# A graph network with cross-attention: a new order of VectorE's steps in the attention units, and of the three engines' steps in the openings

## The reference

```python
h = relu(layernorm(x)); x_in = h
h = batchnorm(h); h = gcn(h, gcn_in_w)              # 1024 nodes, 512 wide, 16384 edges
for i in range(4):
    a = attn(ln2(h), cond, Wq[i], Wk[i], Wv[i], Wo[i])   # 16 batches of 64 nodes, 256 keys each, 8 heads of 64
    h = h + a
    val, gate = split(ln3(h) @ geglu_w[i] + geglu_b[i])
    h = h + (val * gelu(gate)) @ ffo_w[i] + ffo_b[i]
return x + gcn(h, gcn_out_w) + x_in
```

## Time and profile before

| | |
|---|---|
| runs | 2527.58, 2528.76, 2528.82 us; median 2528.76 us |
| profiled execution | 2525.96 us, of which the span from first to last instruction is 2522.8 us |
| mean granted TensorE clock | 0.982 |
| busy: TensorE, its weight loads, VectorE, ScalarE, GpSimd | 2362.4, 2066.8, 1691.1, 1248.3, 1075.6 us |

### The profile page before, as it was taken

How to read it: one execution, slowest core, us unless ns; L and a number is a source line. 1 busy time by engine, 2 the same in 40 slices (tenths; PEclk the granted TensorE clock), 3 DMA queues, 4 the chain that set the end, 5 groups by cost and what they waited for, 6 DMA issues and landing times.

```text
span 2522.8 us, 38407 instructions
## 1 busy us (share of the span) xinstructions
PE 2362.4 (94%) x14270; PEld 2066.8 (82%) x14270; DVE 1691.1 (67%) x3027; ACT 1248.3 (49%) x2585; POOL 1075.6 (43%) x730
## 2 busy tenths in 40 slices
PE   7888899899999999899999999899999999899999
PEld 5367888888888889888888889888887989888887
DVE  9985666676656666686656666686666666686554
ACT  9954656654333555654333555653333555553322
POOL 3136755646643322346643322346553322346530
PEclk9999999999999999999999999999999999999999
DMA  2042333312231333212231333212231333212231
GB/s 76 1 168 89 141 121 121 122 33 69 59 120 45 105 104 118 92 34 67 59 122 51 101 100 118 93 34 67 60 121 58 99 95 118 92 38 63 63 121 42
DMA packets 115880, 214.53 MB, mean 85 GB/s; under 512 B 9520, under 2 KB 71600, under 8 KB 113904
## 3 DMA queue, kind: packets, MB, share of 16 engines
q1 hardware_dynamic: 115408, 207.89, 24.9%
q10 hardware_dynamic: 288, 4.19, 0.4%
HBM read 176.13 MB, written 35.91 MB: 84 GB/s over the span
## 4 chain that ended last, share of the span: by engine, by line
PE 69%; DVE 19%; ACT 6%; issue 4%; POOL 2%; DMA 0%; DVEq 0%; ACTq 0%; POOLq 0%
PE ps L2350 8%; PE ps L2352 8%; PE ps L2351 8%; PE ps L2719 6%; PE ps L2723 6%; PE ps L2721 6%; PE ps L2599 6%; PE ps L2602 6%; PE ps L2601 6%; DVE qbd L2028 2%; DVE kv L2005 2%; DVE o_full L2043 2%; PE ps L2913 1%; PE ps L2627 1%; DVE qbd_b L2028 1%
## 5 line engine op out<-in xcount | busy, mean ns | idle before, releaser
L2599 PE MATMUL ps<-wv_hi,cb 128*128 128x256 f32 x896 | 259.6, 290 | 6.7 <-DVE kv L2005 3.8
L2599 PE MATMUL ps<-cb,wk_hi 128*128 128x256 f32 x896 | 261.3, 292 | 4.6 <-POOL cb L803 2.9
L2601 PE MATMUL ps<-cb,wk_hi 128*128 128x256 f32 x896 | 257.1, 287 | 0.0
L2602 PE MATMUL ps<-cb,wk_lo 128*128 128x256 f32 x896 | 256.7, 286 | 0.0
L2601 PE MATMUL ps<-wv_lo,cb 128*128 128x256 f32 x896 | 256.3, 286 | 0.0
L2602 PE MATMUL ps<-wv_hi,cb 128*128 128x256 f32 x896 | 256.2, 286 | 0.0
L823 POOL TENSOR_TENSOR v_lo<-kv,v_hi 128x512 fp32r<-128x512 f32 x96 | 125.3, 1305 | 292.3 <-ACT v_hi L1260 292.0
L878 POOL TENSOR_TENSOR f_lo<-ff,f_hi 128x512 fp32r<-128x512 f32 x128 | 168.9, 1331 | 172.2 <-ACT f_hi L1504 172.1
L2283 DVE TENSOR_TENSOR h<-h,ps 128x512 f32<-128x512 f32 x256 | 168.3, 683 | 59.7 <-PE ps L2352 59.7
L2352 PE MATMUL ps<-wf_hi,f_lo 128*128 128x512 f32 x512 | 199.2, 389 | 0.0
L2350 PE MATMUL ps<-wf_hi,f_hi 128*128 128x512 f32 x512 | 199.2, 389 | 0.0
(11 more groups left out here) (377 smaller groups left out, 6984.5 us busy)
## 6 DMA issues: line engine op xcount, KB each, us to landing
cb<-cb_s SPq DMA_DIRECT2D x168, 512.0 KB, 4.6
stage<-in_pieces SPq DMA_DIRECT2D x256, 128.0 KB, 2.6
cb_s<-cb SPq DMA_DIRECT2D x56, 512.0 KB, 2.6
stage<-in_pieces SPq DMA_DIRECT2D x44, 512.0 KB, 3.6
stage<-in_condT SPq DMA_DIRECT2D x7, 1024.0 KB, 5.8
stage<-in_pieces SPq DMA_DIRECT2D x16, 256.0 KB, 3.4
at_s<-at_hi ACTq DMA_DIRECT2D x2, 2048.0 KB, 11.7
wo_raw<-in_pieces SPq DMA_DIRECT2D x8, 512.0 KB, 4.6
```

What stands on the lines that cost most here:

```text
L2599: pe.matmul(to, l_hi, r_hi, start=(fresh and i == 0 and k == 0), stop=False, skip_group_check=True)
L2601: pe.matmul(to, l_hi, r_lo, start=False, stop=False, skip_group_check=True)
L2602: last = pe.matmul(to, l_lo, r_hi, start=False, stop=(k == 1), skip_group_check=True)
```

## The change

It moves instructions, and adds or removes none in the groups. Four parts:

1. In the groups VectorE does `q_low` before `kv_five` (before, it did it after `kv_late` 1 and `o_part`), and `pT_low` before the maxima in place of behind them. In the last group `o_low` comes ahead of the reciprocal.
2. In the openings all four `first_x2_low` of both halves are VectorE's. GpSimd's part of them is gone; it waits on `x2_ok` before it takes up its larger pieces.
3. For layers 1 to 3 the sums and the higher part of V1 move from the end of the MLP into the opening (VectorE: ahead of `first_z2` of use 1; ScalarE: behind `q_copy(0, 1)`). In layer 0 the same places hold V0, and GpSimd's lower part of it comes before `kv_low` 1 and 2.
4. On TensorE the last four transposes of use 1 come ahead of key step 5; `kv_late` 1 and 2 follow the lower parts on VectorE.

Besides, in the first graph convolution two of three small copies (`take_picked`) come ahead of the sums of the second key weight.

```diff
 # GpSimd, layer 0, before the layers
-            for j in range(2, BLOCKS):
+            for j in range(2, 5):
+                cond_low(0, j)
+            pool.wait_ge(x2_ok, FIRST)
+            for j in range(5, BLOCKS):
                 cond_low(0, j)
 # GpSimd, opening
-                for k in range(2):
-                    first_x2_low(0, k)
-                kv_low(l, 0, KEYS, 0)
                 first_rsqrt(2 * l + 1)
                 pool.wait_ge(z2_ok, 2 * FIRST * l + 2 * FIRST)
...
+                kv_low(l, 0, KEYS, 0)
                 zero_q()
-                for k in range(2):
-                    first_x2_low(1, k)
+                pool.wait_ge(x2_ok, 2 * FIRST * l + 2 * FIRST)
+                if l == 0:
+                    attn_low(VALUES, 0, 0)
                 for n in range(1, 3):
                     kv_low(l, 0, KEYS, n)
-                if l == 0:
-                    attn_low(VALUES, 0, 0)
                 attn_low(VALUES, 1, l)
 # ScalarE, opening
-                for p in range(1, 3):
-                    q_copy(0, p)
+                q_copy(0, 1)
                 if l == 0:
-                    attn_high(VALUES, 0, 0)
-                q_copy(0, 3)
+                    act.wait_ge(c_lo, BLOCKS)
+                attn_high(VALUES, int(l > 0), l)
+                q_copy(0, 2)
+                act.wait_ge(q_mm, 2 * FIRST * l + FIRST)
                 for k in T2_ORDER[1]:
                     first_x2_high(1, k)
+                q_copy(0, 3)
 # ScalarE, end of the MLP
                     wq_high(l + 1)
-                    attn_high(VALUES, 1, l + 1)
 # VectorE, value_units
                     if t:
+                        q_low(t, 1)
                         o_part(u - 2, 2)
                     kv_five(t, VALUES)
                     kv_11_low(t, VALUES)
+                    pT_low(u)
                     maxima(u + 1)
                     kv_late(t, VALUES, 0)
                     softmax(u + 1)
                     kv_late(t, VALUES, 1)
-                    pT_low(u)
                     if t:
                         o_part(u - 1, 3)
-                        q_low(t, 1)
                     kv_late(t, VALUES, 2)
+                    pT_low(u + 1)
                     maxima(u + 2)
-                    pT_low(u + 1)
 # VectorE, key_units (the same for pT_low)
+                    if last:
+                        o_low(GROUPS * l + t - 1)
                     softmax(u)
-                    if t:
+                    if t and not last:
                         o_low(GROUPS * l + t - 1)
...
                     o_part(u - 2, 0)
                     if not last:
+                        q_low(t + 1, 0)
                         kv_five(t + 1, KEYS)
                     if t:
                         residual(t - 1, GROUPS * l + t - 1)
                     if not last:
                         kv_11_low(t + 1, KEYS)
+                    pT_low(u)
+                    if t:
+                        z3_of(t - 1, GROUPS * l + t - 1)
                     maxima(u + 1)
...
-                        q_low(t + 1, 0)
                         kv_late(t + 1, KEYS, 2)
 # VectorE, opening
-                for k in range(2, KC):
+                for k in range(KC):
                     first_x2_low(0, k)
...
+                attn_sums(VALUES, int(l > 0), l)
                 first_z2(2 * l + 1, range(FIRST))
-                if l == 0:
-                    attn_sums(VALUES, 0, 0)
                 for k in T2_ORDER[1][:3]:
                     first_x2_full(1, k)
-                kv_late(0, KEYS, 1)
+                for k in T2_ORDER[1][:2]:
+                    first_x2_low(1, k)
                 first_x2_full(1, 2)
                 for k in T2_ORDER[1][2:]:
                     first_x2_low(1, k)
-                kv_late(0, KEYS, 2)
-                for i in range(2):
-                    q_low(0, i)
+                for n in range(1, 3):
+                    kv_late(0, KEYS, n)
+                q_low(0, 0)
                 if l == 0:
                     attn_sums(VALUES, 1, 0)
+                q_low(0, 1)
 # VectorE, end of the MLP
-                    if q == MG - 1 and l < L - 1:
-                        attn_sums(VALUES, 1, l + 1)
 # TensorE, opening
                 q_product(0, 3)
-                kv_step(0, KEYS, 5)
                 first_t2(1, T2_ORDER[1][3:])
-                kv_step(0, KEYS, 6)
+                for j in range(5, BLOCKS):
+                    kv_step(0, KEYS, j)
```

More of the change, by code:

```diff
@@ L853, in _ @@
             pool.wait_ge(z2_ok, FIRST)
-            for j in range(2, BLOCKS):
+            for j in range(2, 5):
+                cond_low(0, j)
+            pool.wait_ge(x2_ok, FIRST)
+            for j in range(5, BLOCKS):
                 cond_low(0, j)
             for l in range(L):
-                def first_x2_low(use, k):
-                    pool.wait_ge(full2_ok, 2 * FIRST * l + t2_place(use, k) + 1)
-                    pool.wait_ge(x2_hi_ok, 2 * FIRST * l + t2_place(use, k) + 1)
-                    pool.tensor_tensor(xT2_lo[:, k, :], z3[:, FIRST * use + k, :], bits(xT2_hi[:, k, :]), ALU.subtract)\
-                        .then_inc(x2_ok, 1)
                 def x3_low(t):
@@ L1894, in _ @@
                 at_low(t)
+            for n in range(2):
+                take_picked(0, n)
             attn_sums(KEYS, 1, 0)
-            for n in range(3):
-                take_picked(0, n)
+            take_picked(0, 2)
             def gcn_out(use, t):
@@ L2139, in key_units @@
                         kv_late(t + 1, KEYS, 1)
-                    pT_low(u)
-                    if t:
-                        z3_of(t - 1, GROUPS * l + t - 1)
                     o_part(u - 1, 1)
@@ L2149, in key_units @@
                     else:
-                        q_low(t + 1, 0)
                         kv_late(t + 1, KEYS, 2)
+                    pT_low(u + 1)
+                    if not last:
                         maxima(u + 2)
-                    pT_low(u + 1)
-                    if last:
+                    else:
                         o_part(u + 1, 3)
```

## The result

The kernel after takes 2432.26 us (median of four runs, 2431.05 to 2433.99) against 2528.61 us: a ratio of 0.962, 95% interval 0.9604 to 0.9637. That is 96.4 us less; 85 us were forecast, and the time lies in the range given. The profiled execution took 2431.27 us, its span is 2429.5 us, 93.3 us shorter than before, and its mean granted clock 0.991 in place of 0.982. TensorE is busy for 96% of the span.

A forecast was written before the change was run, and what follows sets the result against it. The kernel was taken as matmul work with short holes, TensorE carrying 69% of the wait chain. Terms 19 + 9 + 14 + 18 - 2 + 14 + 7 + 6 = 85 us gave 2444 us, forecast range 2424 to 2464.

The forecast's parts named there:

- Value units, groups 1 to 6 of layers 1 to 3: Waits for q_low of about 1.05 us each go, kv_five stays covered, oT_lo's chain moves along: 19 us gained.
- rival (a): The wait moves: ScalarE's chain to oT_lo, or exp behind later maxima, sets the groups; 2481 us, chance 0.22.
- Key units: Groups 1 to 6, layers 1 to 3: 0.85 us wait goes, step 6 waits about 0.4 us; 9 us gained, 0 to 15.
- First key unit of layers 1 to 3: Early q_low avoids GpSimd's wo_lo: 3.1 us of wait and 1.4 of clock go, three times; 14 us gained.
- Groups 1 to 6 of layer 0: Value wait of 2 us becomes 1 us, the clock stays up, key wait of 0.8 us goes; 18 us, 8 to 21.
- First group of layer 0: 0.6 us lost at value step 6, kv_five 3.3 us late in the key unit: -2 us, -3.5 with clock.
- Last group: Each layer: q_low's 1.4 us go, early o_low cuts output wait from 2.5 to 1.1 us; 14 us, 6 to 18.
- Openings of layers 1 to 3: z2 wait goes as V1 sums leave the MLP tail; key step 6 waits 3.1 us; 7 us gained, 0 to 13.
- Opening of layer 0: x2_low wait falls from 3.4 to 0.9 us, V1's lower part ends earlier; 6 us gained, 3 to 8.

The follow-up runs named there:

- `pT_low` back: Kernel after, but in groups 0 to 6 of every layer pT_low stands behind the maxima and z3_of behind kv_late 1, as before: 2427.01 us, 0.9595.
- `q_low` three times: Kernel after, but in value units of groups 1 to 7 of layers 1 to 3 VectorE does q_low three times in a row: 2473.51 us, 0.9784.
- the groups alone: Kernel before with only the new order of VectorE's value_units and key_units, all openings as before: 2454.34 us, 0.9707.
- `q_low` alone: Kernel before with only q_low moved early; pT_low, z3_of, o_low and the openings as before: 2455.7 us, 0.9711.
- V1 back: Kernel after, but the sums and higher part of weights V1 stay at the MLP's end for layers 1 to 3: 2443.24 us, 0.9665.

## Why the prediction held, step by step

**Value units, groups 1 to 6 of layers 1 to 3: right.** The waits for the queries went and `kv_five` stayed covered. 22.1 us for 19, since with them 1.23 us a group went and not 1.05: the row of the wait gives 0.98 us of idle time, but the score product started 1.58 us after its transposes did, and starts 0.36 us after them now. `kv_five` has 1.3 us of cover for the 0.7 of the slow `q_low`, which did not come. oT_lo's chain moved along, as the step said; it stops TensorE for 0.29 us. So rival (a) did not come.

**Key units: right.** A new wait of 0.32 us at step 6, 8.6 us for 9. The run with `pT_low` back shows the cause that the step named, `pT_low` and `z3_of` ahead of the maxima, by taking them away: the wait goes.

**First key unit of layers 1 to 3: right**, 14.2 us for 14, the clock's share included.

**Groups 1 to 6 of layer 0: right.** 18.6 us for 18. `kv_five` waits 0.5 to 0.9 us where 1 us was said, and the clock no longer falls. The row that decides is `q_low` beside GpSimd, 2.86 us at 294.28. The Trainium skill (SBUF — State Buffer, "SBUF: two separate sides") has VectorE's instructions with two SBUF inputs and GpSimd's reading ones wait for each other for a whole instruction; this case agrees: in the run with `q_low` three times one half took 2.44 us beside GpSimd's `w_lo` pieces of some 2.5 us each, and 0.42 us without.

**First group of layer 0: right sum, wrong place.** The prediction had `kv_five` late by 3.3 us in the key unit. In after it is 0.98 us, because TensorE had already lost 4.3 us at value step 6, where 0.6 us more than before was forecast. The 0.6 us are right: step 6 comes 7.75 us after the raw sum, and 7.14 before. The rest of that wait is TensorE's reaching it 2.2 us sooner, reckoned from the raw sum. In the second trace of the same kernel the two waits are 1.64 and 3.08 us, close to what was said, and the sum is -4.1 us. Both waits hang on the same chain from the raw load, and that the first trace's sum met the forecast is in part luck.

**Last group: right**, 3.84 us each in three layers and 2.45 in layer 3, where the clock fell. The wait for oT_lo is 0.97 us for 1.1. That `o_low`'s place is what counts is read from the row in which it stands behind the reciprocal; no run moves it apart from `pT_low` and `z3_of` of that group. The prediction took waits of this size as too short for the clock to fall. That it held in three of the four here is luck: over the ten traces here with this order of the last group and no copies of `q_low`, the waits in it are 1.5 us and less, and the clock fell in 18 of 40 last groups, which then took 1.3 to 3.9 us more. With the groups alone all four fell and the term was 7.0 us.

**Openings of layers 1 to 3: mechanism right, size off, 11.9 us for 7.** The wait for z2 went because of the sums of V1, as the run that puts them back shows. Key step 6 waits 2.90 us for 3.1 and the query product 0.60 for 1. Most of what is missing lies in the first half, up to the first query product. It is in layer 1, before and after:

```profile
765.38:780.16 14.78, 11.87 (x77) 11.67 (x77) 12.17 (x24) 3.72 (x6) 3.54 (x3) 0.77 0.00 1
```

```profile
739.09:748.78 9.69, 9.09 (x77) 8.88 (x75) 8.57 (x15) 3.73 (x6) 0.00 (x0) 1.00 0.01 2
```

That is 5.1 us for the 2.8 forecast, with a granted clock of 0.77 before and 1.00 after; layers 2 and 3 give 3.6 and 3.7, 12.4 us in all for 8.4. Three things make the difference. The prediction's own figures, 2.9 + 1.4 - 1, are 3.3 us and not 2.8; the query product waits 0.4 us less than it said; and the fall of the clock behind the wait for z2, priced at 1.4 us, cost 2.8 in layer 1.

The second half gave -0.6 us for -1.5, as a balance of falls of the clock that the term did not hold. Its 0.5 us are the waits alone (3.1 against 2.19 and 0.4); the fall that it names beside the 3.1 has no price in it. In after the clock falls behind key step 6's wait in layers 1 and 3, which costs 1.3 and 2.7 us. Before, it fell behind the second wait in layers 2 and 3. The 48 matmuls of the second half's query products in layers 1 and 2, before:

```profile
798.95:809.97 11.02, 11.02 (x48) 9.12 (x49) 6.35 (x5) 3.99 (x8) 5.84 (x3) 1.00 0.01 2
1363.70:1376.33 12.63, 12.63 (x48) 10.28 (x49) 6.34 (x5) 3.98 (x8) 5.82 (x3) 0.86 0.00 0
```

The same wait of 2.19 us stands ahead of both; behind the second the granted clock is 0.86 and 1.6 us are lost. I had looked at layer 1 alone.

**Opening of layer 0: right by one trace**, 5.8 us for 6, and 8.0 in the second trace, at the end of the range of 3 to 8. And some of it is not the opening's. The key steps of layer 0 start at 178.49 us in after and at 179.54 before, since in the trace before TensorE waited 1.72 us in the first graph convolution for one of the small copies (`xs_c`), and does not after. The prediction had no term for these copies, and that their new place gave this is not shown: with the groups alone and with `q_low` alone the copies stand where they were and the wait is absent too. What differs is the time of the sums ahead of the copy, here the first of them, before and with the groups alone:

```profile
157.08 1.52 DVE L1714 TENSOR_TENSOR sums_s<-stage 128x256 f32<-128x256 f32 x1
```

```profile
158.12 0.41 DVE L1714 TENSOR_TENSOR sums_s<-stage 128x256 f32<-128x256 f32 x1
```

From the first key step to the raw sum it is 53.5 us before, 48.8 and 47.1 in the two traces of after: 4.7 and 6.4 us.

## What to carry to other kernels

Where a hand-ordered engine makes an operand just in time, look for the hole in its own list that lies earlier, and check two things there: what stands behind it and how much cover that has, and what the other engine on the same memory does at that moment. One move, `q_low`, was worth as much as the whole new order of the groups; the moves that came with it cost 0.46 us a group in layers 1 to 3 and made a last group 2.3 to 6.1 us shorter, clock included, so test such parts apart. Read every repeat of a stage, not one, before a stall is priced: two of three openings hid another 1.6 us. And take a second trace of the same kernel before a term of a few us is called right: two terms of this sum moved by 2.2 us between two traces.

## What the hardware did that I had not expected

After the same wait the clock falls in one place and not in another. Key step 6 of the openings in layers 1 and 2, after, at and behind a wait of 2.90 us each:

```profile
766.09:768.82 2.73, 2.73 (x12) 2.73 (x13) 0.00 (x0) 0.61 (x1) 1.28 (x1) 0.50 0.03 6
1309.65:1311.17 1.52, 1.52 (x12) 1.52 (x13) 0.00 (x0) 0.61 (x1) 0.77 (x1) 1.00 0.00 0
```

Twelve matmuls at a granted clock of 0.50, the level of 1.2 GHz, take 2.73 us, and at 1.00 1.52. Over nine traces the clock fell behind 23 of 33 such waits of 2.9 to 3.0 us, and behind none of the 11 waits of 1.5 to 1.6 us that the edits made of them. For layers 1 to 3 the places were the same in both traces of after; in most of the other kernels they were others, but with `kv_five` ahead of `o_part` and with V1 back the same two openings fell. By the traces this moves a kernel's time by some 5 us either way without regard to what the edit does (an estimate: falls in the openings cost 1.3 to 2.8 us each, in the last groups 1.3 to 3.9), as much as the edits of a few us that were tested here; what decides it was not found out.
